# Causal attention: softmax reciprocals turned once a tile and spread by fp32r products, values scaled in SBUF

## What is computed

```python
# B, S, EMB = 2, 1024, 256; NQ, NKV, D = 16, 4, 64; g = NQ // NKV
q = _rotary((x @ Wq + bq).reshape(b, s, NQ, D))
k = _rotary((x @ Wk + bk).reshape(b, s, NKV, D))
v = (x @ Wv + bv).reshape(b, s, NKV, D)
logits = jnp.einsum('bqhgd,bkhd->bhgqk', q.reshape(b, s, NKV, g, D), k) * scale
w = jax.nn.softmax(jnp.where(causal, logits, -1e30), axis=-1)
out = jnp.einsum('bhgqk,bkhd->bqhgd', w, v).reshape(b, s, NQ * D)
return out @ Wo + bo
```

## Time and profile before

| | |
|---|---|
| median of 3 runs | 1623.82 us (1622.97 to 1626.99) |
| profiled execution, its own time | 1621.63 us |
| its span, first to last instruction | 1619.9 us |
| mean granted TensorE clock | 0.904 of full speed |
| busy in the span | PE 84%, DVE 51%, ACT 41%, POOL 31% |

### The profile page before, as it was taken

One profiled execution on the slowest core, in us unless ns is written; L12 is line 12 of the kernel. 1 busy time (PEld: TensorE's weight loads), 2 busy tenths in 40 slices (PEclk: granted clock), 3 DMA queues, 4 the chain that ended last, 5 costly groups with the idle time before them and its releaser, 6 DMA issues. The chain is left out here.

```text
span 1619.9 us, 25645 instructions
## 1 busy us (share of the span) xinstructions
PE 1353.0 (84%) x8239; PEld 916.4 (57%) x8240; DVE 822.2 (51%) x1601; ACT 658.9 (41%) x1905; POOL 507.7 (31%) x592
## 2 busy tenths in 40 slices
PE   7888599545898999999889999994999438999980
PEld 3544388423655666666656666663787434666650
DVE  1288578776444544554345555552677751222225
ACT  3498244211455555555355556550334101222212
POOL 0055212244233412420453222000122424555534
PEclk9999699755999999999999999997999558999995
DMA  9000000000111000000100001004300101111114
GB/s 289 1 1 1 0 1 0 1 0 1 40 27 27 15 14 14 14 14 14 27 14 14 15 14 40 1 1 192 120 1 0 53 7 39 43 45 45 45 36 156
DMA packets 36134, 56.01 MB, mean 35 GB/s; under 512 B 6528, under 2 KB 27392, under 8 KB 36032
## 3 DMA queue, kind: packets, MB, share of 16 engines
q1 hardware_dynamic: 32288, 44.47, 9.2%
q0 software_dynamic: 3744, 10.23, 1.9%
HBM read 34.90 MB, written 9.31 MB: 27 GB/s over the span
## 5 line engine op out<-in xcount | busy, mean ns | idle before, releaser
L1636 DVE TENSOR_REDUCE ga_neg_top<-ps 128x1 f32<-128x128 f32 (+7 forms) x256 | 181.8, 752 | 132.3 <-PE ps L1374 132.3
L1383 PE MATMUL ps<-ident,ga_e 128*128 128x128 f32 x1152 | 190.7, 284 | 8.5 <-DVE ga_att L1654 3.9
L1502 ACT ACTIVATE ga_e<-ps,ga_neg_top 128x128 f32<-128x128 f32 (+7 forms) x256 | 188.0, 741 | 16.5 <-DVE ga_neg_top L1636 15.7
L1399 PE MATMUL ps<-ga_e_tr,ga_v 128*64 128x256 f32 x1152 | 167.5, 400 | 24.8 <-DVE ga_att L1654 13.4
L1511 ACT COPY ga_e_tr<-ps 128x512 f32<-128x512 f32 (+3 forms) x192 | 91.9, 479 | 193.5 <-PE ps L1383 192.0
L1383 PEld LDWEIGHTS ps<-ident,ga_e 128*128 128x128 f32 x1152 | 123.7, 142 | 82.7 <-issue 62.5
L195 POOL COPY x_nat<-tail_xn 128x256 f32<-128x256 f32 (+1 forms) x80 | 31.7, 397 | 406.5 <-DVE tail_xn L226 406.5
L2066 PE MATMUL ps<-ex_gate_up,ex_scratch 128*128 x312 | 141.8, 598 | 0.6 <-ACT ex_scratch L2099 0.6
L1644 DVE COPY ga_e_tr<-ps 128x128 f32<-128x128 f32 (+3 forms) x192 | 101.9, 552 | 42.6 <-PE ps L1383 41.3
L188 POOL TENSOR_TENSOR tail_rstd<-tail_var_eps,neg_half 128x1 f32<-128x1 f32 x80 | 52.7, 658 | 213.4 <-DVE tail_var_eps L216 213.4
L1399 PEld LDWEIGHTS ps<-ga_e_tr,ga_v 128*64 128x64 f32 x1152 | 68.4, 137 | 71.1 <-issue 30.1
(11 more groups left out here) (286 smaller groups left out, 2794.4 us busy)
## 6 DMA issues: line engine op xcount, KB each, us to landing
ga_q_swapped<-ga_q_raw SPq DMA_DIRECT2D x64, 128.0 KB, 2.3
ex_gate_up<-in_ex_gate_up SPq DMA_DIRECT2D x1, 8192.0 KB, 23.2
ex_down<-in_ex_down SPq DMA_DIRECT2D x1, 4096.0 KB, 34.8
x_tr<-in_x_tr SPq DMA_DIRECT2D x4, 512.0 KB, 6.8
x_nat<-in_x SPq DMA_DIRECT2D x1, 2048.0 KB, 11.7
ga_k_swapped<-ga_k_raw SPq DMA_DIRECT2D x16, 128.0 KB, 2.3
xn_rows<-x_tr SPq DMA_DIRECT2D x8, 256.0 KB, 2.1
x_tr<-choice_rows SPq DMA_DIRECT2D x8, 256.0 KB, 5.5
```

The costliest lines, as they stand in the source:

```text
L1383: last = nc.tensor.transpose(ps_tr[n % 2][:, (kb - k0) * P:(kb - k0 + 1) * P], e[half][t % 2][:, kb * P:(kb + 1) * P], core.ident[:])
L1399: last = nc.tensor.matmul(ps_att[half * HD:(half + 1) * HD, :], v[:, v_slot(b, kb), kv * HD:(kv + 1) * HD], e_tr[g % 2][:, kb, half, :], s ...
L1502: nc.scalar.activation(e[half][t % 2][:, 0:blocks(t) * P], ps_scores(t, half), ACT.Exp, bias=neg_top[t % 2][:, half:half + 1], accum_out=s ...
L1636: nc.vector.tensor_reduce(neg_top[t % 2][:, half:half + 1], ps_scores(t, half), AX.X, ALU.max, negate=True).then_inc(top_ready, 1)
```

## The change

The reciprocals of a whole tile are handled together. `sums` and `recip` become 16 columns wide (one for each head), and DVE inverts them once a tile, at i = 0 of the next one. PE then transposes `recip` into bank 7 (`turn_recip`, i = 1): 16 rows of 128 queries. ACT copies these rows to fp32r (`rows_to_high`, the high half), DVE writes what the rounding left over to the rows 32 to 47 (`rows_to_low`). A constant `pick` (one 128 x 128 weight for each pair, ones where a row of high or low belongs to the head) spreads them: `spread_recip(J, part)` makes four fp32r products into bank 7, part 0 at i = 2 and part 1 at i = 3. The values are copied unscaled out of `ps_att` by ACT (`copy_values`, at the place where it copied `recip_all`), and DVE multiplies half a tile at a time (512 columns) in SBUF by bank 7 (`normalise(J, part)`, one step after each spread). `weigh_values` now waits for `att_copied`.

To make room in bank 7 other users are moved: key pieces to i = 0 and 1, value pieces to steps 48, 72, 80 and 88, `tail_xn` to i = 7 (three steps after the projection), the turned-back transpose to i = 0. Two setup operations on DVE make `pick` and clear `recip_rows`.

```diff
-            if t in (start, start + 2):
-                return m, (t - start) // 2
+            if t in (start, start + 1):
+                return m, t - start
-    V_STEPS = {6 * QT + 1: 4, 9 * QT: 5, 9 * QT + 1: 6, 9 * QT + 2: 7}
+    V_STEPS = {6 * QT: 4, 9 * QT: 5, 10 * QT: 6, 11 * QT: 7}
     def normal_at(t):
-        if t == END + 2:
-            return TILES - 1
-        return out_at(t - 5) if t < END else None
+        return out_at(t - 3)
     def turned_back_at(t):
-        return normal_at(t - 2)
+        return out_at(t - 4)
+    def rows_at(t):
+        return out_at(t + 3)
+    def spread_at(t):
+        for part in range(2):
+            if out_at(t + 2 - part) is not None:
+                return out_at(t + 2 - part), part
+        return None
...
# PE
-                        need(pe, att_done, g)
+                        need(pe, att_copied, g)
...
-                def spread_recip(g):
-                    pe.wait_ge(recip_ready, g + 1)
-                    for i in range(2):
-                        for half in range(2):
-                            n = 2 * i + half
-                            last = nc.tensor.matmul(ps_recip[half * HD:(half + 1) * HD, i * P:(i + 1) * P],
-                                                    recip[:, n:n + 1].to_broadcast([P, HD]), core.ident[:], start=True, stop=True)
-                    last.then_inc(recip_all_ready, 1)
+                def turn_recip(J):
+                    take_piece_bank((rows_low, J + 1))
+                    pe.wait_ge(recip_ready, J + 1)
+                    nc.tensor.transpose(ps_piece[0:2 * QT, 0:P], recip[:], core.ident[:]).then_inc(rows_ready, 1)
+                def spread_recip(J, part):
+                    take_piece_bank((att_done, 2 * J + part + 1))
+                    pe.wait_ge(rows_low, J + 1)
+                    for i in range(QT // 2):
+                        last = nc.tensor.matmul(ps_piece[:, i * P:(i + 1) * P], pick[:, part * QT // 2 + i].rearrange("p i d -> p (i d)"),
+                                                recip_rows[:], start=True, stop=True)
+                    last.then_inc(spread_ready, 1)
                 def project_out(J, part):
-                    pe.wait_ge(att_done, QT // 2 * (J + 1))
+                    pe.wait_ge(att_done, 2 * J + part + 1)
...
# ACT
+                def copy_values(g):
+                    J, first = divmod(2 * g, QT)
+                    act.wait_ge(att_ready, g + 1)
+                    if J >= 2 and first == 0:
+                        act.wait_ge(tail.y_ready, tail.base + J - 1)
+                    nc.scalar.copy(att[J % 2][:, first:first + 2, :].rearrange("p r t -> p (r t)"), ps_att).then_inc(att_copied, 1)
+                def rows_to_high(J):
+                    act.wait_ge(rows_ready, J + 1)
+                    need(act, spread_ready, 2 * J)
+                    nc.scalar.copy(recip_rows[0:2 * QT, :], ps_piece[0:2 * QT, 0:P]).then_inc(rows_high, 1)
...
-                        nc.scalar.copy(recip_all[:], ps_recip).then_inc(recip_all_copied, 1)
+                    if group_at(t, 5) is not None:
+                        copy_values(group_at(t, 5))
+                    if rows_at(t - 1) is not None:
+                        rows_to_high(rows_at(t - 1))
...
# DVE, at the start of a step where normalise stood
+                def normalise(J, part):
+                    half = slice(part * QT // 2, (part + 1) * QT // 2)
+                    dve.wait_ge(spread_ready, 2 * J + part + 1)
+                    dve.wait_ge(att_copied, QT // 2 * J + QT // 4 * (part + 1))
+                    values = att[J % 2][:, half, :].rearrange("p r t -> p (r t)")
+                    nc.vector.tensor_tensor(values, values, ps_piece, ALU.mult).then_inc(att_done, 1)
+                def rows_to_low(J):
+                    dve.wait_ge(rows_high, J + 1)
+                    nc.vector.tensor_tensor(recip_rows[32:32 + 2 * QT, :], ps_piece[0:2 * QT, 0:P], recip_rows[0:2 * QT, :].bitcast(F32),
+                                            ALU.subtract).then_inc(rows_low, 1)
...
+                    if spread_at(t - 1) is not None:
+                        normalise(*spread_at(t - 1))
+                    if rows_at(t - 1) is not None:
+                        rows_to_low(rows_at(t - 1))
```

More of the change, by code:

```diff
@@ L1215, in stage_causal_attention @@
         e_tr = [core.sb(ctx, f"ga_e_tr{i}", [P, SEQ_TILES, 2, 2 * P]) for i in range(2)]
-        sums = [core.sb(ctx, f"ga_sums{i}", [P, 4]) for i in range(2)]
-        recip = core.sb(ctx, "ga_recip", [P, 4])
-        recip_all = core.sb(ctx, "ga_recip_all", [P, 2 * P])
+        sums = [core.sb(ctx, f"ga_sums{i}", [P, 2 * QT]) for i in range(2)]
+        recip = core.sb(ctx, "ga_recip", [P, 2 * QT])
+        recip_rows = core.sb(ctx, "ga_recip_rows", [P, P], F32R)
+        pick = core.sb(ctx, "ga_pick", [P, QT, 2, HD], F32R)
         att = [core.sb(ctx, f"ga_att{i}", [P, QT, P]) for i in range(2)]
@@ L1436, in _ @@
                         transpose_chunk(t - 1, i)
-                    if g is not None and second:
-                        spread_recip(g)
                     if out_at(t) is not None:
@@ L1452, in _ @@
                         project_v(V_STEPS[t])
+                    if rows_at(t) is not None:
+                        turn_recip(rows_at(t))
+                    if spread_at(t) is not None:
+                        spread_recip(*spread_at(t))
                     if turned_back_at(t) is not None:
@@ L1672, in _ @@
                             copy_chunk(t - 1, i)
-                    if group_at(t, 3) is not None:
-                        invert_sums(group_at(t, 3))
+                    if rows_at(t + 1) is not None:
+                        invert_sums(rows_at(t + 1))
                     if variance_at(t) is not None:
```

47 lines of the change are left out of this document (18 added, 29 removed).

## The result

The changed kernel takes 1583.06 us in the median (1578.78 to 1585.49, six runs) against 1622.61 us (1620.52 to 1626.99, six runs) of the kernel before on the same chip: a ratio of 0.9752, 95% interval 0.9734 to 0.9769. The profiled execution took 1582.28 us, 39.35 less than that of before, where the sum said 26.8.

The account below looks back on a forecast made before the run. PE's issue, plus a few PE waits, was taken to bound the attention stage. Terms -11 - 3.5 - 19 + 5.3 + 1.4 = -26.8 us from 1621.63 gave 1594.8, with 2.2 for the median 1597.0; range 1585 to 1613.

Parts of the forecast that it names:

- Part 1: Spreading on PE: 64 calls removed, one transpose and two spreads added per tile; -11 us, bounds -18 and +3.
- Part 2: ACT and DVE: values' bank free after ACT's copy, shortening ten PE waits; -3.5 us, bounds -6 and 0.
- Part 3: `tail_xn` at i=7: stalls at steps 27, 51, 75 and 76 go; -19 us, bounds -20 and -14.
- Part 4: Shared bank: ten PE waits of 0.87 at i=0 and 1, less 3.4 of old waits; +5.3 us.
- Part 5: The end: after the last values two spreads and two wider products alternate; +1.4 us.
- (a): Spreads: fp32r products are dear, Part 1 worth nothing or costing up to 3; 1608 to 1611 us, chance 0.12.
- (b): POOL's chain only shifts: `tail_xn` waits for rstd or tile 9's query rotation is late; 1607 us, chance 0.10.
- (e): Stall at the key casts stays whole because something else holds POOL; +19, 1616 us, chance 0.06.
- (c): Same-step bank waits bring ACT's and DVE's whole step, 2 us each instead of 0.87; +11, 1608 us, chance 0.11.
- (d): PE waits for ACT and DVE at turned rows and both spreads, 48 waits; +42, 1639 us, chance 0.06.

Follow-up runs that it names:

- twice: The changed kernel with the four fp32r products of each spread issued twice; 1595.88 us, ratio 0.9839.
- norm: The kernel before with one edit, `tail_xn` moved to i=7; 1605.11 us, ratio 0.9896.
- mid: The changed kernel with key and value projections moved to the middle of a step, their copies earlier on ACT and DVE; 1569.97 us, ratio 0.9684.
- arith: The changed kernel with the old places of key pieces, value pieces, `tail_xn` and turned-back transpose; 1608.77 us, ratio 0.9925.
- low_f32: The changed kernel with four further plain f32 products, 64-column weights on the lower columns, ahead of each spread; 1616.07 us.
- up_f32: The changed kernel with four further plain f32 products, 64-column weights on the upper columns, ahead of each spread; 1614.62 us.
- full_f32: The changed kernel with four further f32 products with full 128-column weights ahead of each spread; 1604.99 us.

## Why the prediction was wrong

**Part 1** is the step that failed: fewer products on an engine that bounds the stage was right as a mechanism, but three prices of its sum were wrong, all in the same direction. The call was put at 0.59 us, from its first load to the next scores, as read at step 122 (i=2). It is worth that there, where scores stand behind it, but 0.77 at i=4 and 6: between full-width work the gap of 0.17 us *ahead* of its first load, which stood in the same row, goes with it too. I took both gaps for "the gap of a wait", a thing that any work there would have, and so charged one to the turn and one to each spread as well. The turn was put at 0.38 and costs 0.11 (one instruction, no gap), a spread at 0.63 and costs 0.40. Per tile 2 x 0.18 + 0.27 + 2 x 0.23 = 1.09 us, in 15 tiles 16.4. That is more than the 12.6 us by which the sum missed; the drain (1.8 more than forecast) and the time outside the stage (3.4) took part of it back. The price of 0.116 for a full-width fp32r product was good (0.11 by `twice`). PE instructions fell by 368 and not 352, because the turn is one and not two. The row that contradicted my reading was at hand: in the earlier trace rows transposes with no wait ahead of them have a gap too, behind the values. The lower bound of -18 rested on cheaper products, not on the gap, and so was not low enough.

**Part 2** was right, -4.0 for -3.5.

**Part 3** was right in cause, place and size: -19.0 in the changed kernel, and -19.4 at the three stalls by `norm` alone (-17.9 over all its steps, with step 68 at the lower clock).

**Part 4** was right: ten waits at the ten named places, 0.78 for 0.87 each, and `mid` gives back 8.2 us in those ten steps when they are taken away. Its credit was 4.0 where I had 3.4.

**Part 5** had the alternation of spreads and products right in kind, but not the fall of the clock that lengthened the projection behind it: +3.2 for +1.4.

**The rivals.** (a) is refuted by `twice`, (b) and (e) by the windows of steps 27, 51 and 75, (c) by the waits of 0.78. (d), 48 waits at the turned rows and spreads, did not come: in the changed kernel PE waits for DVE at one spread alone, the last one in the drain, 0.8 us. But `arith` shows its mechanism where the bank's next user stands in the same step: there 14 waits cost 11.3 us.

## What to carry to other kernels

Read the gaps on *both* sides of a group of products, and ask which work stands before and behind it, before calling them a wait: a short group of plain f32 products with weights of 64 columns between full-width ones costs its own time and two gaps, and its removal, or its widening, gives them back; where other work of another division stands behind it, only one of them. Order work of the same division together; the cost of a change is read from start to start of the products, not from the loader's idle time. When one bank serves several users, two of them in one step cost the evacuation of the first, here 0.78 us, unless other work of PE is put between them.

## What the runs showed of the hardware

Eight f32 instructions with 64-column weights took 0.41 us of loads when they alternated between the column halves, and 0.85 us when all were in one half (`low_f32` and `up_f32` alike), about as long as eight of 128 columns (0.81 us from start to start of the products in `full_f32`). Four fp32r ones in the lower half added only 0.24 us behind the spread and 0.29 ahead of it. A transpose of f32 is one instruction where an f32 product is two. I had expected none of these.

The rule on loads that I weighed (the Trainium skill, "TensorE: Matmul & The Clock Gate", section "LDWEIGHTS (loading the stationary operand)") counts a load's columns at 1.2 GHz, 0.053 us for 64. The alternating products agree with it, 0.051; those in one half, 0.106 each, do not. So the columns of a load don't set the pace there; what does, no run shows.
